# A gelu one sub-step later, and a value projection ahead of the expert products, in a two-layer gated cross-attention and mixture-of-experts kernel

## The reference, cut to what matters

```python
x = x + tanh(g_xattn[0]) * L0_xattn(layernorm(x), ctx, ctx)
x = x + tanh(g_ffn[0])   * L0_ffn(layernorm(x))       # 8 experts of 512, gelu (erf), top 2
x = x + tanh(g_xattn[1]) * L1_xattn(layernorm(x), ctx, ctx, mask)
x = x + tanh(g_ffn[1])   * L1_ffn(layernorm(x))       # 8 experts of 64 + one shared
# attention: softmax(q k^T / sqrt(8)) v over 1500 keys, 16 heads
# experts:   y = gelu(x W1 + b1) W2 + b2, weighted by the gate, summed
```

## Time and profile before

| | |
|---|---|
| median of 3 runs | 1040.72 us (1039.66 to 1044.62) |
| the profiled execution: its time | 1040.23 us |
| the profiled execution: its span | 1038.1 us |
| mean granted clock of PE over the span | 0.981 of full |
| PE busy | 922.5 us (89%) |
| DVE busy | 723.0 us (70%) |
| ACT busy | 586.2 us (56%) |
| POOL busy | 525.0 us (51%) |

### The profile page before, as it was taken

How to read it: one execution, slowest core, us unless ns; L and a number is a source line. 1 busy time by engine, 2 the same in 40 slices (tenths; PEclk the granted TensorE clock), 3 DMA queues, 4 the chain that set the end, 5 groups by cost and what they waited for, 6 DMA issues and landing times.

```text
span 1038.1 us, 32346 instructions
## 1 busy us (share of the span) xinstructions
PE 922.5 (89%) x13088; PEld 675.9 (65%) x13088; DVE 723.0 (70%) x1531; ACT 586.2 (56%) x1060; POOL 525.0 (51%) x667
## 2 busy tenths in 40 slices
PE   2487899999999999999999999999999999999974
PEld 0154577777777777777777777666666666666753
DVE  3376576785767768586785867878787878787722
ACT  1044556556565565656547565665757575757560
POOL 5353445543546335453446565665657576672202
PEclk9998899999999999999999999999999999999995
DMA  8735653333323333233465646767676767665200
GB/s 181 133 90 137 145 126 72 72 83 69 63 55 85 70 77 76 37 81 70 95 137 88 143 110 132 162 123 156 124 152 122 145 130 146 137 137 97 52 2 18
DMA packets 95215, 107.24 MB, mean 103 GB/s; under 512 B 22394, under 2 KB 86972, under 8 KB 95068
## 3 DMA queue, kind: packets, MB, share of 16 engines
q1 hardware_dynamic: 95068, 105.19, 49.0%
HBM read 35.89 MB, written 0.46 MB: 35 GB/s over the span
## 4 chain that ended last, share of the span: by engine, by line
PE 66%; DVE 16%; ACT 9%; issue 5%; SPq 2%; DMA 1%; POOL 0%; POOLq 0%; ACTq 0%; DVEq 0%
PE pO L993 13%; PE pMX L1010 12%; PE pST L972 12%; PE pKV L1124 6%; PE pFY L1082 6%; PE pKV L1115 5%; PE pFH L1150 5%; DVE mx L925 4%; DVE mx L920 4%; ACT P L678 3%; DVE rden L839 3%; PE pFY L1047 2%; ACT HR L715 1%; PE pFY L1086 1%; ACT V L696 1%
## 5 line engine op out<-in xcount | busy, mean ns | idle before, releaser
L678 ACT ACTIVATE P<-pST 125x448 f32<-125x448 f32 x768 | 396.1, 542 | 349.9 <-PE pST L972 344.3
L925 DVE TENSOR_REDUCE mx<-pMX 112x1 f32<-112x500 f32 x384 | 258.4, 673 | 172.3 <-PE pMX L1010 172.1
L1010 PE MATMUL pMX<-kop,qmax 104*112 104x500 f16 x768 | 293.1, 392 | 44.7 <-DMA qmax<-qlo 18.5
L972 PE MATMUL pST<-qexp,kop 106*128 106x112 f16 (+1 forms) x3072 | 280.2, 214 | 19.9 <-ACT P L678 9.3
L972 PEld LDWEIGHTS pST<-qexp,kop 106*128 106x128 f16 (+1 forms) x3072 | 209.9, 102 | 127.1 <-issue 42.9
L920 DVE TENSOR_REDUCE mx<-pMX 112x1 f32<-112x500 f32 x384 | 255.8, 666 | 42.8 <-PE pMX L1010 41.9
L993 PE MATMUL pO<-P,V 125*17 125x112 f32 x6144 | 186.0, 262 | 0.0
L993 PEld LDWEIGHTS pO<-P,V 125*17 125x17 f32 x6144 | 136.8, 98 | 46.2 <-issue 36.3
L1010 PEld LDWEIGHTS pMX<-kop,qmax 104*112 104x112 f16 x768 | 99.0, 132 | 93.1 <-issue 21.7
L563 POOL CAST khi<-kfull 128x500 f16<-128x500 f32 x96 | 57.7, 601 | 193.0 <-ACT kfull L691 192.8
L565 POOL TENSOR_TENSOR klo<-kfull,khi 128x500 f16<-128x500 f32 x96 | 109.0, 1135 | 7.8
(11 more groups left out here) (144 smaller groups left out, 1089.6 us busy)
## 6 DMA issues: line engine op xcount, KB each, us to landing
C<-in_ctxT SPq DMA_DIRECT2D x32, 750.0 KB, 6.2
kop<-khi SPq DMA_DIRECT2D x192, 125.0 KB
kop<-maskop SPq DMA_DIRECT2D x48, 437.5 KB
kop<-klo SPq DMA_DIRECT2D x96, 125.0 KB
qexp<-qmax SPq DMA_DIRECT2D x32, 182.0 KB
maskin<-in_mask SPq DMA_DIRECT2D x8, 656.2 KB, 6.2
kop<-maskop SPq DMA_DIRECT2D x2, 1312.5 KB
qmax<-qhi SPq DMA_DIRECT2D x128, 7.0 KB
```

Of the source, the lines that this page charges most:

```text
L678: nc.scalar.activation(P[0:KP, slot, h * 4 * T:(h + 1) * 4 * T], pST[0:KP, h, 0:4 * T], ACT.Exp, scale=EXP_SCALE).then_inc(exp_done, 1)
L925: nc.vector.tensor_reduce(mx[:, s % 2, m // PAIRS, m % PAIRS:m % PAIRS + 1], pMX[0:T, 1, 0:CW], AX.X, ALU.max).then_inc(max_done, 1)
L972: mm = nc.tensor.matmul(pST[0:cols, h, i * T:(i + 1) * T], kop[0:ROWS, b, p, tile * KP:tile * KP + cols], qexp[0:ROWS, b, p, :, :].rearran ...
L1010: nc.tensor.matmul(pMX[0:T, m % 2, 0:CW], qmax[0:SHIFT0, st.s % 2, p, :, :].rearrange("r j q -> r (j q)"), kop[0:SHIFT0, st.s % 2, p, c * ...
```

## The change

On ACT, in the steps with `has_f(s)`, the gelu moves from the end of sub-step 8 to the end of sub-step 9, behind the exponentials (9, 0) and (9, 1) and the evacuation of `v1`. In the same steps, at kt 10, the evacuation of `v2` moves ahead of exponential (10, 0). On PE, in the same steps at kt 10, the projection `v2` moves from between the two halves of the scores to ahead of `y0`. The code of the projection and of the evacuation is put into functions, `project` and `evacuate`, and is otherwise the same. No instruction is added or removed, no operand changes, and all semaphore counts stay as they are.

```diff
@@ scalar engine, step(st)
-                for kt in range(KT):
-                    exps(st, kt, 0)
+                def evacuate(kt):
+
                     for use in [u[1] for u in kv_uses(s) if u[0] == kt]:
                         c = int(use[1])
                         act.wait_ge(kv_ready, st.at(lambda s: upto(kv_uses, s, use)))
...
+                for kt in range(KT):
+                    if has_f(s) and kt == 10:
+                        evacuate(kt)
+                    exps(st, kt, 0)
+                    if not (has_f(s) and kt == 10):
+                        evacuate(kt)
                     exps(st, kt, 1)
...
-                    if kt == 8 and has_f(s):
+                    if kt == 9 and has_f(s):
                         act.wait_ge(fh_free, st.at(lambda s: before(fh_uses, s + 1, True)))
@@ tensor engine, step(st)
+                def project(kt):
+
+                    for use in [u[1] for u in kv_uses(s) if u[0] == kt]:
+                        c = int(use[1])
+                        free(kv_free, kv_uses, use)
...
+                        else:
+                            l = layer_of(s)
+                            for i in range(KPC):
+                                first = (KPC * c + i) * KP
+                                rows = min(KW, S2 - first)
+                                cols = slice(first, first + rows)
+                                for k, (x_, m) in enumerate(((Chi, Whi), (Chi, Wlo), (Clo, Whi))):
+                                    mm = nc.tensor.matmul(pKV[0:rows, i * D:(i + 1) * D], x_[:, s % 2, cols], m[:, l, 1, :],
+                                                          start=(k == 0), stop=(k == 2))
+                        mm.then_inc(kv_ready, 1)
...
                     experts = [u[1] for u in fy_uses(s) if u[0] == kt and early(u[1])]
                     if experts:
+                        project(kt)
                         small("y0")
...
-                    for use in [u[1] for u in kv_uses(s) if u[0] == kt]:
...
+                    if not experts:
+                        project(kt)
                     if has_m(s) and not experts:
                         max_scores(st, MAXES_PER_KT * kt + 1)
                     score_half(st, kt, 1)
```

More of the change, by code:

```diff
@@ L1030, in free @@
                         pe.wait_ge(sem_, st.at(n))
+                def project(kt):
+                    for use in [u[1] for u in kv_uses(s) if u[0] == kt]:
+                        c = int(use[1])
+                        free(kv_free, kv_uses, use)
+                        if use[0] == "k":
+                            if s == -1:
+                                pe.wait_ge(init_c, 2 * LAYERS + c + 1)
+                            else:
+                                pe.wait_ge(ctx_split, st.at(lambda s: CH * s + c + 1))
+                            b, l, cols = (s + 1) % 2, layer_of(s + 1), slice(c * CW, (c + 1) * CW)
+                            for i, (m, x_) in enumerate(((Whi, Chi), (Whi, Clo), (Wlo, Chi))):
+                                mm = nc.tensor.matmul(pKV[:, 0:CW], m[:, l, 0, :], x_[:, b, cols],
+                                                      start=(i == 0), stop=(i == 2))
+                        else:
+                            l = layer_of(s)
[7 more added lines that the diff above has]
+                        mm.then_inc(kv_ready, 1)
                 def early(use):
```

## The result

| | before | after |
|---|---|---|
| median | 1042.12 us (1039.66 to 1044.62, 4 runs) | 1064.23 us (1062.49 to 1066.82, 4 runs) |
| profiled execution: time, span | 1040.23, 1038.1 us | 1066.82, 1065.0 us |
| mean granted clock | 0.981 | 0.965 |
| layer-0 period at full clock | 63.30 us | 64.17 us |
| layer-1 period, steps with a mask | 55.38 us | 56.29 us |

The ratio is 1.0214, 95% interval 1.0177 to 1.0251: 22 us slower, where 8.4 were forecast. The forecast for the steps of layer 0 came out to a hundredth of a microsecond, yet the time lies 10 us outside the range. The profiled execution is the slowest of the four, and that of the kernel before is among its fast ones, so the two lie 26.9 us apart; what follows splits up these 26.9.

A forecast was written before the change was run, and what follows sets the result against it. PE, busy 922.5 us, was taken to bound the kernel. Layer 0 (6.9), layer 1 (1.0) and step 32 (0.5) add 8.4 us to 1040.23: 1048.6; with the median 0.5 higher, 1049.1, stated as 1049.0, range 1043.5 to 1054.

The forecast's parts named there:

- The gelu's shift: Layer 0, ACT: behind three more instructions the gelu starts at 235.49, 1.52 us later, and y0 shifts equally.
- the wait ahead of `y0`: Layer 0, PE: waits 2.0 us for the gelu after v2, where before it waited 1.17.
- `v2` hidden in it: Layer 0, PE: the projection v2, 0.66 us, runs from 234.65 to 235.3, inside the wait for the gelu.
- the waits for exponential (10, 0): Layer 0, behind y1: score (11, 0) waits for this exponential and goes at 242.11, 1.23 us late.
- the period of layer 0 at full clock: Layer-0 groups lie 64.2 us apart instead of 63.33; each of eight steps costs 0.86, 6.9 us in all.
- the reload ahead of its wait: ACT: the second table load runs ahead of the exponential's wait for scores; otherwise the sum grows by some 12 us.
- score (11, 1) of layer 1: Layer 1, behind y1: these scores go at 734.77 against 734.60, 0.17 us later.
- the sum: Whole kernel: 6.9 for layer 0, 1.0 for layer 1 and 0.5 for step 32 make 8.4 us.
- rival 3: PE's longer layer-0 wait brings half clock: up to 3 us a fall, up to 1073 us in all; chance 0.08.
- step 32 by its order alone: Step 32, with no projection to fill the wait and no maximum, was taken to cost 0.5 us.
- A term mis-sized: layer 1: Layer 1, steps 20 to 30: six steps at +0.17 us each, +1.0 us in all.
- gets all its work from PE: DVE in PE's later waits for maxima, 4.5 us over seven steps: they move along and swallow none of the shift.

The follow-up runs named there:

- The pair with waits of 2.7 us: Gelu alone moved to the end of sub-step 9, against the kernel before: 1068.3 us; that kernel with v0's matmuls made twice: 1084.3 us.

## Why the prediction was wrong

**Right.** The gelu's shift (1.52 forecast, 1.53 seen), the wait ahead of `y0` (2.0; 1.93), `v2` hidden in it, the waits for exponential (10, 0), the period of layer 0 at full clock (64.2; 64.17), the reload ahead of its wait, score (11, 1) of layer 1 up to the combination of the maxima (0.17; 0.12). The load shows no drain in either kernel: 1.31 us in the earlier trace rows, 239.22 to 240.53 after.

**Right by luck.** The changed kernel with its waits filled stands 8 us above the kernel before, and the sum says 8.4. Its parts do not agree so well: 6.94 in layer 0 (forecast 6.9), 4.63 in layer 1 (1.0), 0.73 in step 32 (0.5), together 12.3.

**The step that failed: rival 3.** The sum has no term for the clock; it stands in rival 3 alone. The bracket was there, 1.17 us without a fall and 2.5 with one, and 2.0 between them. It got 0.08 and should have been near even, for nothing in the rows spoke for the one end. What the runs showed in its place: four falls in layer 0 (1.66 us each, about half of the 3 that I allowed), and one that I had not looked for, in step 32, where nothing fills the wait and the tail stays at half clock: 5.4 us. I had priced step 32 by its order alone (0.5). The order alone, with the wait of step 32 filled, cost 0.5 and 0.7 there in two traces. Together the falls are 12 us, and filling the waits gave 12.6 back.

**A term mis-sized: layer 1.** Forecast 6 × 0.17 = 1.0, measured 4.7, nearly all of it in the five steps with a mask (0.91 each). The sentence that failed is that DVE "gets all its work from PE", so that later waits move along. DVE's time also hangs on what POOL does at that moment, and POOL, which works through the mask and the three splits without a pause, did not shift with PE. With the collision removed a step costs 0.12, near the forecast 0.17.

**Open.** What decides whether a given wait is followed by a fall. The pair with waits of 2.7 us and the two steps 32 with waits of 0.72 show that it is not the length alone. The experiments do not go further. Nor is it known where the other executions of the kernel before lost clock: they took up to 1047.1 us, at a mean granted clock down to 0.970, and none of the slower ones was traced.

## What to carry to other kernels

A wait of PE has two prices: its own length, and the half clock that may follow; where the second cannot be excluded from rows at both ends, give it a real chance, and look at the tail, where a fall is never made good. If PE must wait, work of no use in the wait can be worth more than it costs. A move that looks closed within one engine changes which instructions of the others meet: look at DVE's short instructions on SBUF tensors beside POOL's long ones.

## What the runs showed of the hardware

- PE's granted clock fell to 1.2 GHz behind waits of 1.93 us in some steps and not in others of the same kernel; eight waits of 2.7 us in a row brought no fall at a period of 64.8 us, and half of them did at 65.5; in step 32 a wait of 0.72 us was followed by one in one kernel and not in another. Eight waits of 1.3 us brought none. A short fall in layer 0 cost 1.66 us.
- DVE's combination of the maxima is two instructions of 0.17 us each where POOL is idle. One took 1.03 us (L910) and the other 3.29 (L909), and each ended within 0.03 us of POOL's instruction. In the kernel before L902, the same as L909, took 0.41 and ended 0.02 us behind POOL's Chi (735.23 to 735.83), and L903, which started 0.02 us ahead of Clo, was not held. The Trainium skill ("GPSIMD Engine Reference", section "Specifications") says that GpSimd's SBUF interfaces are shared with VectorE, with contention for DVE instructions in a 2-port mode or with two SBUF inputs; "SBUF — State Buffer", section "SBUF: two separate sides", calls it an exclusive lock for the whole instruction. L910, with two SBUF inputs, agrees. L909 has one tensor input, and no run here shows in which mode it ran.
